# A fused attention and gated-MLP layer: the causal mask of the row maxima moved to GpSimd, rotation moved to GpSimd, maxima transposed together

## What is computed

```python
h = _layernorm(x) * (1 + ca) + sa
q, k, v = h @ Wq + bq, h @ Wk + bk, h @ Wv + bv       # 16 query heads, 4 key heads, d = 16
q, k = _rope(q), _rope(k)                             # rotation of pairs by cos, sin
scores = einsum('bhgnd,bhsd->bhns', qg, k) / sqrt(d)
att = softmax(where(tril, scores, -inf))              # causal
y = einsum('bhns,bhsd->bhnd', att, v).transpose(...).reshape(B, T, C // g)
x = x + ga * (y @ Wo + bo)
h = _layernorm(x) * (1 + cb) + sb
# routed block: h1 = rmsnorm(h); h + (h1 @ wv + bv) @ wo; rmsnorm; silu(gate) * up; down
x = x + gb * where(sigmoid(h @ w_router + b) > 0.5, processed, h)
```

## Time and profile before

| | us |
|---|---|
| median of 3 runs (lowest, highest) | 476.27 (476.25, 476.64) |
| the profiled execution | 478.08 |
| its span, from the first to the last instruction | 476.4 |
| PE busy with matmuls | 438.0 (92%) |
| DVE busy | 354.8 (74%) |
| ACT busy | 293.8 (62%) |
| POOL busy | 228.1 (48%) |

### The profile page before, as it was taken

How to read it: one execution, slowest core, us unless ns; L and a number is a source line. 1 busy time by engine, 2 the same in 40 slices (tenths; PEclk the granted TensorE clock), 3 DMA queues, 4 the chain that set the end, 5 groups by cost and what they waited for, 6 DMA issues and landing times.

```text
span 476.4 us, 9453 instructions
## 1 busy us (share of the span) xinstructions
PE 438.0 (92%) x3320; PEld 372.0 (78%) x3320; DVE 354.8 (74%) x771; ACT 293.8 (62%) x596; POOL 228.1 (48%) x296
## 2 busy tenths in 40 slices
PE   1986789978999999899999999999999999999994
PEld 1774455776677779788857999999889699999994
DVE  5479987679998359999875989897756646587461
ACT  1169369686668765636597774556858778655350
POOL 6285835740452560304656534446343546366244
PEclk9999799999999999999999999999999999999998
DMA  6904012000000000110030000010002001002011
GB/s 188 308 19 134 8 32 66 2 0 2 1 2 30 0 1 2 48 43 2 3 96 1 23 1 1 2 56 3 1 3 68 0 1 46 2 2 56 0 45 45
DMA packets 16448, 16.04 MB, mean 34 GB/s; under 512 B 4105, under 2 KB 14798, under 8 KB 16402
## 3 DMA queue, kind: packets, MB, share of 16 engines
q1 hardware_dynamic: 16402, 15.43, 10.4%
HBM read 11.09 MB, written 4.21 MB: 32 GB/s over the span
## 4 chain that ended last, share of the span: by engine, by line
PE 77%; DVE 11%; ACT 4%; issue 3%; POOL 2%; DMA 1%; SPq 1%; POOLq 0%; ACTq 0%; DVEq 0%
PE banks L789 8%; PE banks L790 8%; PE banks L791 8%; PE banks L705 7%; PE banks L717 6%; PE banks L578 5%; PE banks L579 5%; PE banks L580 5%; PE banks L679 5%; PE banks L658 4%; DVE mxp L1168 3%; DVE mx L1168 2%; PE banks L668 2%; ACT QKT L906 2%; PE banks L772 1%
## 5 line engine op out<-in xcount | busy, mean ns | idle before, releaser
L789 PE MATMUL banks<-gTh,guhi 128*128 128x256 f32 x352 | 101.2, 288 | 0.7 <-DVE V L1130 0.7
L791 PE MATMUL banks<-gTh,gulo 128*128 128x256 f32 x352 | 98.7, 280 | 0.0
L790 PE MATMUL banks<-gTl,guhi 128*128 128x256 f32 x352 | 98.7, 280 | 0.0
L926 ACT ACTIVATE PT<-banks 128x1024 f32<-128x1024 f32 (+3 forms) x96 | 74.8, 809 | 33.8 <-PE banks L705 31.5
L789 PEld LDWEIGHTS banks<-gTh,guhi 128*128 128x128 f32 x352 | 66.4, 189 | 1.9 <-DVE gTl L1240 1.0
L790 PEld LDWEIGHTS banks<-gTl,guhi 128*128 128x128 f32 x352 | 66.4, 189 | 0.3
L791 PEld LDWEIGHTS banks<-gTh,gulo 128*128 128x128 f32 x352 | 66.3, 188 | 0.0
L1168 DVE TENSOR_REDUCE mxp<-banks 128x2 f32<-128x1024 f32 (+3 forms) x56 | 61.4, 1139 | 5.0 <-PE banks L684 3.6
L679 PE MATMUL banks<-QKT 128*128 128x512 f32 (+3 forms) x192 | 51.3, 373 | 9.1 <-ACT QKT L906 5.9
L705 PE MATMUL banks<-QKT 128*128 128x512 f32 (+3 forms) x192 | 50.8, 367 | 1.4 <-DMA QKT<-wo_mr 0.5
L705 PEld LDWEIGHTS banks<-QKT 128*128 128x128 f32 x192 | 30.8, 189 | 21.3 <-issue 18.1
(11 more groups left out here) (176 smaller groups left out, 1131.3 us busy)
## 6 DMA issues: line engine op xcount, KB each, us to landing
xres<-in_L_attn_x SPq DMA_DIRECT2D x8, 512.0 KB, 3.8
out_x<-xres SPq DMA_DIRECT2D x8, 512.0 KB, 2.9
wm_st<-in_L_wmod SPq DMA_DIRECT2D x1, 1024.0 KB, 9.8
modB<-mod_scratch SPq DMA_DIRECT2D x4, 256.0 KB, 3.4
wg_st<-in_L_ffn_w_gate SPq DMA_DIRECT2D x1, 704.0 KB, 5.6
wu_st<-in_L_ffn_w_up SPq DMA_DIRECT2D x1, 704.0 KB, 6.7
xres<-in_L_ffn_w_down SPq DMA_DIRECT2D x1, 640.0 KB, 6.1
wm_st<-in_L_wmod SPq DMA_DIRECT2D x1, 512.0 KB, 6.2
```

Of the source, the lines that this page charges most:

```text
L789: pe.matmul(out_, guhi[:, k, blk, :], gh, start=(m == 0 and k == 0), stop=False)
L790: pe.matmul(out_, guhi[:, k, blk, :], gl, start=False, stop=False)
L791: i = pe.matmul(out_, gulo[:, k, blk, :], gh, start=False, stop=(m == len(blocks) - 1 and k == KB - 1))
L926: act.activation(PT[:, u % 2, 2 * q:2 * q + 2, 0:CH - q0], both("prob", b, n)[:, :, 0:CH - q0], ACT.Exp, scale=float(D) ** -0.5).then_inc( ...
```

## The change

Four things change, and with them the whole of `ORDER`.

1. The mask of the maxima leaves PE. The matmuls at L684 go. A new step `dcp` (ACT) copies the diagonal block of each of the 12 diagonal units from PSUM to a new buffer `own` in SBUF; `msel` (POOL) masks a tile's 128x512 elements there with one `affine_select`, and `mxd` (DVE) reduces them. `mxr` now leaves the diagonal block out, and is not needed at all for the units that are nothing but a diagonal block (18 instead of 20 a batch). It waits for `dcp` of the same unit where there is one. `own` has room for two tiles, so `dcp` waits for `mxd` of two tiles before.
2. `rope` and `stlo` are the same instructions, now on POOL. `rot` is no buffer of its own any more but lies in `qk`, so `qkvb` of the next chunk waits for `sthi` and `stlo` instead of `rope`.
3. The maxima lie in `mt32`, 32 columns for each tile, so that `mtT` is one transpose of 128x128 for four tiles. `mrow` then takes four copies of 8x128 instead of one of 8x512.
4. PE starts with 14 matmuls of `ident` with itself (`WARM`) into a bank that nobody reads yet.

`ORDER` is written anew throughout. The staging buffers of two weights now lie in `zbuf`.

```diff
+WARM = 14
...
-DVE_STEPS = dict(wts=1, wob=1, wol=1, biasq=1, stats=NC, qkvb=NJ, rope=NC, stlo=NC, mxr=NM, mneg=NC, ytm=NC, x1=NJ,
+DVE_STEPS = dict(wts=1, wob=1, wol=1, biasq=1, stats=NC, qkvb=NJ, mxr=len(OTHER), mxd=NT, mneg=NC, ytm=NC, x1=NJ,
...
-POOL_STEPS = dict(rstd1=NC, norm1=NT, pmask=ND, rstd2=NJ, hmod=NJ, rs1=NJ, rs2=NJ, ffl=NJ, fin=NJ)
+POOL_STEPS = dict(msel=NT, rstd1=NC, norm1=NT, rope=NC, stlo=NC, pmask=ND, rstd2=NJ, hmod=NJ, rs1=NJ, rs2=NJ, ffl=NJ, fin=NJ)
...
-ldx ldx stats pzero asetw asetb setw vkeys pmodc vmodc setb rstd1 norm1 norm1 xT4 norm1 bias6 xev wts qkv4 norm1 xT5
+ldx ldx pzero stats setw pmodc vmodc setb asetw wts stats rstd1 norm1 norm1 norm1 norm1 xT4 xT5 xev qkv4 rstd1 norm1
...
+                elif kind == "msel":
+
+                    wait("dcp", OWN_END[n])
+                    tile = own[:, n % 2].rearrange("p e q k -> p (e q) k")
+                    pool.affine_select(out=tile, in_=tile, compare_op=ALU.is_ge, fill=NEG, base=0,
+                                       pattern=[[0, H], [-1, P]], channel_multiplier=1).then_inc(S["msel"], 1)
...
+            pe.wait_ge(s_const, C_IDENT)
+            for _ in range(WARM):
+                pe.matmul(bank(7)[:, 0:P], ident[:], ident[:], start=True, stop=True)
...
-                    if diag:
-                        for e in range(2):
-                            i = pe.matmul(o[:, e, 0:len(at) * kn].rearrange("p (m k) -> p m k", k=kn)[:, :, kn - P:kn],
-                                          ident_b[:], mask_qk[:].unsqueeze(1).to_broadcast([P, len(at), P]),
-                                          start=False, stop=True)
...
-                    for t in range(TPC):
-                        i = pe.transpose(o[0:2 * H, t * P:(t + 1) * P],
-                                         mt[:, n * TPC + t, :, :].rearrange("p h e -> p (h e)"), ident[:])
-                    i.then_inc(S["mtT"], 1)
+                    pe.transpose(o[:, 0:P], mt32[:, n * TPC:(n + 1) * TPC, :].rearrange("p t n -> p (t n)"), ident[:]
+                                 ).then_inc(S["mtT"], 1)
...
+                elif kind == "dcp":
+                    u = OWN[n]
+                    qt, _, kn, at = MAX_UNITS[u]
+                    wait("max", u + 1)
+                    if qt >= 2:
+                        wait("mxd", qt - 1)
+                    else:
+                        earlier("mxd", NT + qt - 1)
+                    o = both("max", b, u)[:, :, 0:len(at) * kn].rearrange("p e (m k) -> p e m k", k=kn)
+                    act.activation(own[:, qt % 2, :, at[0]:at[-1] + 1, :], o[:, :, :, kn - P:kn], ACT.Copy
+                                   ).then_inc(S["dcp"], 1)
...
+                    for t in range(TPC):
+                        i = act.activation(mrT[:, t * P:(t + 1) * P], of("mtT", b, n)[32 * t:32 * t + 2 * H, 0:P], ACT.Copy)
+                    i.then_inc(S["mrow"], 1)
...
+                    if u in OWN:
+                        wait("dcp", OWN.index(u) + 1)
...
+                elif kind == "mxd":
+                    wait("msel", n + 1)
+                    dve.tensor_reduce(mxp[:, n, :, :, 2], own[:, n % 2], AX.X, ALU.max).then_inc(S["mxd"], 1)
```

More of the change, by code:

```diff
@@ L97, in released @@
         return "ycopy", P_UNITS[n][0] + 1
-    by = dict(bias="biasq", xT="xev", qkv="qkvb", stack="stk", max="mxr", mtT="mrow", prob="exp", yT="ytm", ynT="ynev",
+    if kind == "max":
+        return ("mxr", OTHER.index(n) + 1) if n in OTHER else ("dcp", OWN.index(n) + 1)
+    by = dict(bias="biasq", xT="xev", qkv="qkvb", stack="stk", mtT="mrow", prob="exp", yT="ytm", ynT="ynev",
               wo="x1", hT="hlo", a="route", h2T="h2lo", down="sum")
@@ new lines @@
+exp hhi ms1 route pmask pmask xT4 norm1 hlo rs1 norm1 ms2 ms2 pv pv qkvb qkv3 qkvb rope wob a5 ycopy yT6 xev qkv7 xT4
+xev ytm ynT6 ynev sthi a2 route ms2 rs2 h2 h2 route ms2 wo6 x1 wo5 qkv4 wts stlo stack0 qkvb qkvb woh wol stack2 stk
+stk max0 max6 h2T4 dcp h2hi x1 rstd2 norm2 h2lo dcp mxr rs2 h2 rope sthi msel msel mxd mxd max2 dcp mxr max0 dcp mxr
+h2 gate4 stlo msel rstd2 max6 dcp mxr mxd max2 dcp mxr msel mxd h2T0 sil h2hi h2lo stack6 stack2 gate5 stk stk mneg
+mtT1 max6 mrow mrd ldx ldG ldW norm2 mxr max2 max6 mxr dcp hmod ms1 hmod msel max0 mxr max2 mxr rs1 norm1 ms1 norm1
```

230 lines of the change are left out of this document (114 added, 116 removed).

## The result

The changed kernel takes **488.12 us** (median of 4 runs, 486.44 to 490.04) against 476.26 us for the kernel before in the same session: a ratio of 1.024, 95% interval 1.0216 to 1.0266. It is slower by 11.9 us; forecast were 7 us less, and the range ended at 481. The profiled execution took 489.72 us with a span of 488.0, so it is 1.6 us above the median.

What follows compares the result with a forecast made beforehand. PE was taken as the bound after a start paced by others. PE -7.3, DVE -4 and start +4 sum to -7.3 us: 470.8 for the profiled execution, 469.0 for the median; range 461 to 481.

Steps and rivals of the forecast that it cites:

- PE -7.3: On PE: removed mask matmuls 6.7 us and fewer transposes 3.1 us, a quarter not counted for the first batch; -7.3 us.
- DVE -4: On VectorE: rotation and low parts leave, net busy time about -30 us, worth -4 us between 0 and -12.
- start +4: First batch: rotation behind the gates on POOL makes the second chunk's transposed maxima 4.6 us later; +4, between +1 and +7.
- step-by-step count of 48.6: First batch: walking POOL's and ACT's steps put the second chunk's first transposes near 48.6 us instead of 40.81.
- a matmul less on PE is worth its spacing in the second regime: From about 120 us on PE works almost without a gap, so a removed matmul saves its distance to the next start.
- the 30 us of the count: VectorE's busy time: 33 us leave, reductions shrink 4.6, extra maxima add 5.5; net about -30 us, to near 325.
- Two engines at one port, 0: VectorE's two-input SBUF instructions held up beside a busier POOL: left at zero, +2 us at the upper end.
- The moved rotation: Rotation on POOL: 4.1 us a chunk, priced in the first batch only; in three batches POOL has the room.
- The third, 486.6 us: Rival: longer way from score to maximum through ACT, POOL and DVE, 13 us for seven chunks; 486.6 us, slower 0.25.

Runs made afterwards that it cites:

- after_fourth_pair_early: Kernel after with the first batch's start slightly reordered (third projection ahead of the masked products) and the gates' six instructions on VectorE; 487.1 us, ratio 1.0222 to before.
- before_no_mask: Kernel before without its 96 mask matmuls, so the maxima cover all keys of the block; 474.8 us, ratio 0.9972 to before.
- after_rope_quarter: Kernel after with the rotation on GpSimd working on one tile of four, same places and waits; 485.3 us, ratio 1.0171 to before.
- after_bare: Kernel after without masked copies, selection and extra maxima, rotation and low parts on GpSimd for one tile of four; 486.2 us, ratio 1.0196 to before.
- before_rope_pool: Kernel before with rotation and low parts moved to GpSimd at their old places in the order; 500.6 us, ratio 1.0514 to before.
- before_bare: The work of after_bare on the same engines, in the order of the kernel before; 480.5 us, ratio 1.0076 to before.

## Why the prediction was wrong

**It went to the wrong side.** By its own terms: PE -7.3, DVE -4, start +4.

*The start, +4.* The number is right, the mechanism only in part. The second stack came 4.7 us later (3 us earlier than my step-by-step count of 48.6, since the first chunk's rotation began at 20.50, not 23.2), the second transposed maxima at 70.88, where I had 70. But I had the gates on POOL hold the second rotation. It does start behind them and two `msel`:

```profile
37.16 1.23 POOL L576 TENSOR_SCALAR_AFFINE_SELECT own<-own 128x512 f32<-128x512 f32 x2
38.37 0.72 POOL L562 TENSOR_TENSOR stk<-qk,cos_t 128x256 f32<-128x256 f32 x1
```

But what it reads is written only at 37.61, by VectorE, because the chunk's last projection runs on PE 5.4 us later than before:

```profile
35.21 1.57 PE L704 MATMUL banks<-Wq_b,xTc 128*128 128x192 f32 x8 [1.57 <-ACT xTc L923]
```

```profile
37.26 0.35 DVE L1185 TENSOR_TENSOR V<-banks,bias_q 128x64 f32<-128x64 f32 x2
```

Before:

```profile
29.84 1.46 PE L658 MATMUL banks<-Wq_b,xTc 128*128 128x192 f32 x8
```

POOL's queue thus adds 0.8 us, and with the gates taken off it, in after_fourth_pair_early, the rotation starts no earlier. That the gates ended just when the operand was ready is luck for the count. What stood behind the second maxima was counted too low: with the first output projection at 79.73 the first batch is 7.8 us late (71.88 before). 2.4 us of that is a wait of PE for a VectorE instruction that follows on the 3.66 us one shown first; beside that one POOL has the instruction shown second:

```profile
75.59 3.66 DVE L1144 TENSOR_TENSOR Wo_l<-wo_mr,Wo_h 64x256 fp32r<-64x256 f32 x1
```

```profile
75.36 3.60 POOL L528 TENSOR_TENSOR wdlo<-xres,wdhi 128x1536 fp32r<-128x1536 f32 x1
```

*PE, -7.3.* The step that failed is "a matmul less on PE is worth its spacing in the second regime". It rested on PE being 97% busy. The size of what is removed was about right: without the masks PE is busy 6.2 us less. But PE isn't a queue of work that closes up when an entry is taken out; in before_no_mask 4.0 us came back as idle time. Measured, the masks are worth 1.3 us by the medians and 2.2 by the rest, and the transposes nothing: a fifth to a third of the term.

*DVE, -4.* Measured on three quarters of the rotation: 2.3 us by the medians; from the second stack on, 0.2. And the relief was smaller than the 30 us of the count: DVE's busy time fell by 11.3 us. By form, after (busy, mean ns; the last three against 482, 875 and 456 ns before):

```profile
L1200 DVE TENSOR_REDUCE mxp<-own 128x4 f32<-128x512 f32 x32 | 21.2, 679 | 0.4 <-POOL own L576 0.2
...
L1248 DVE TENSOR_SCALAR hbuf<-xres,mv,rstd 128x256 f32<-128x256 f32 x32 | 21.1, 699 | 6.0 <-PE banks L810 5.3 <-POOL rstd L481 0.6
...
L1144 DVE TENSOR_TENSOR Wo_l<-wo_mr,Wo_h 64x256 fp32r<-64x256 f32 x4 | 6.2, 1558 | 0.0
...
L1228 DVE TENSOR_TENSOR ytm<-ytm 128x256 f32<-128x256 f32 x8 | 6.0, 752 | 0.3
```

The extra maxima cost what was counted (0.68 each; the count left out a join of the first chunk's maxima, 0.9 us in all). Most of the 18.5 us between 325 and 343.5 are instructions that became longer: 7.0 us in the second normalization, 2.7 in L1144, 2.4 in L1228, and smaller amounts in six more forms.

*Two engines at one port, 0.* This is the term that was mis-sized for DVE's busy time: I left it at zero with +2 at the end of the range. The durations of the second normalization after, least, median, most:

```profile
L1248 DVE TENSOR_SCALAR hbuf<-xres,mv,rstd x32: 381/414/1485, 83.9 to 439.3; 128x256 f32<-128x256 f32 x32
```

The median is as it was (408), the mean 0.2 us more: it takes 0.41 us where POOL is idle and up to 1.49 where it is in an instruction of its own. Before, 22 of the 32 had no POOL instruction beside them, after 11. That isn't only the rotation's doing: the mean is 663 ns in after_rope_quarter and 646 in after_bare, but 483 in before_rope_pool, where POOL has the whole rotation. It is the order that sets normalizations beside POOL's work. The section of the Trainium skill that the prediction named ("SBUF — State Buffer", "SBUF: two separate sides") says that the lock takes in a VectorE instruction in a two-port mode too, and not only one with two inputs; the trace fits, since L1248 has one tensor as input and is stretched beside GpSimd; in which mode it runs the trace doesn't say. I had looked for two-input instructions alone.

*The moved rotation.* This is the other step that failed, a term put at nothing. I had priced its length (4.1 us a chunk; 4.5 measured, low parts 1.5) at the start only and nothing later, because POOL "has the room". Room in the mean isn't a free queue when the operand comes. In the old order the length costs 12.1 us of the rest, in the new order 5.0 by the profiles and 2.8 by the medians.

*The rivals.* The third, 486.6 us, has the number but not the mechanism: it laid 13 us on the way from score to maximum, and without that way the new order is no faster. What I should have had is a rival of this form: the new order with its new placement needs longer for the same work. As far as the runs divide the 11.6 us of the span: 4.7 at the start; in the rest 2.8 to 5.0 for the rotation's length; and the last 1.9 to 4.1, to which the masks' 2.2 come if they were gained as in the old order, between the mask's way, the low clock and the order, which the runs don't part. The executions profiled scatter by some 2 us, so these are sizes, not sums to a tenth. before_bare and after_bare say that the order has a share that no added work explains, 2.6 to 5.7 us for bare work.

*What stays open*: which places of the new order lose it. The trace of the kernel after shows no single wait of that size (PE's largest is the 6.67 us at the second stack, and none behind it is longer than 2.5 us); its idle time is longer than before in each of the stretches from 60 us to the end. And whether the new placement with some third order would beat the kernel before is not shown by any run. None of the 18 kernels computes everything and is faster than the kernel before beyond its interval.

## What to carry to other kernels

Where several engines run fixed queues, an order and a placement are one thing: moving a step to a less busy engine costs that engine's queue at that very place, so read the timeline of the *receiving* engine where the operand becomes ready, not its mean load. A PE that is 97% busy need not finish earlier by what is taken from it: take it away in an experiment before counting it. When several parts change at once, compare the same reduced work in both orders; undoing parts one at a time did not price them here. And work put back for such a comparison needs places of its own: one reduction at the place of a copy made a wait of 3.1 us.

## What the runs showed of the hardware

- A VectorE instruction of 128x256 elements with a single tensor as input takes 0.38 to 0.41 us with no GpSimd instruction beside it and up to 1.49 with one, and a two-input one of 64x256 elements took 3.66 us, ending 0.3 us after a GpSimd instruction that had begun 0.2 us before it.
- 36 and 28 short matmul entries in two pauses (4.25 and 3.29 us) kept the granted clock at 1.00 over a stretch where it was 0.61, and the sixteen transposes behind the first took 1.94 us instead of 3.65, with no effect on the median and 2.4 us on the profiled span.
- The low parts take 0.71 and 0.62 us on VectorE and 0.76 on GpSimd in the mean, but the shortest on VectorE take 0.41 and on GpSimd 0.73: the means are close only because VectorE's are held up beside GpSimd. Rotation products take 0.48 to 0.69 us on VectorE and 0.73 to 0.79 on GpSimd in the mean, and at least 0.41 and 0.71; on a quarter of the elements 0.21 and 0.31.
